# GNN stack on one core: one-hots of a message group in two halves, left-overs added one step later

## What is computed

```python
s = s @ (w_lin1_s / sqrt(MUL)); v = einsum('nui,uw->nwi', v, w_lin1_v / sqrt(MUL))
w = silu(edge_scalars @ fc_w1') @ fc_w2'          # w0, w1, w2, w3: 32 columns each
se = s[edge_src]; ve = v[edge_src]; es = edge_attr[:, :1]; ev = edge_attr[:, 1:4]
mid_s0 = w0 * se * es
mid_s1 = w3 * einsum('eui,ei->eu', ve, ev) / SQRT3
mid_v0 = (w1 * se)[:, :, None] * ev[:, None, :]
mid_v1 = (w2 * es)[:, :, None] * ve
ns = segment_sum(concat([mid_s0, mid_s1]), edge_dst); nv = segment_sum(concat([mid_v0, mid_v1]), edge_dst)
```

## Time and profile before

| what | us |
|---|---|
| median of 3 runs (8615.7 to 8623.8) | 8616.8 |
| profiled execution, own time | 8619.5 |
| span of its records | 8617.7 |
| message pass, from the first group's products to the last reduce | 1300 to 2353 |
| busy in the span: POOL / DVE / PE / ACT | 6169 / 5708 / 5622 / 3353 |
| mean granted TensorE clock, share of full | 0.76 |

### The profile page before, as it was taken

The page is one execution under the profiler, slowest core; times in us unless marked ns, Lnnn a source line. Parts: engine busy times, 40 slices in busy tenths (PEclk is TensorE's granted clock), DMA queues, the critical chain, the costliest instruction groups (busy, mean ns, idle before and its releaser), DMA issues. The chain is left out here.

```text
span 8617.7 us, 105909 instructions
## 1 busy us (share of the span) xinstructions
PE 5622.0 (65%) x23206; PEld 3921.9 (46%) x23206; DVE 5707.8 (66%) x15405; ACT 3352.8 (39%) x10636; POOL 6169.0 (72%) x6427
## 2 busy tenths in 40 slices
PE   5576646666666665777766666666655555788885
PEld 3343323444344443444444444444444444666664
DVE  8938308888866666666666666555544444788987
ACT  2232326777645553333323343000001111566665
POOL 2878767777577776777777777777777777666664
PEclk6555557777788888999989998788865555788886
DMA  2111115443322223444444443644433332211111
GB/s 71 46 57 46 54 62 142 112 113 109 90 76 63 64 63 108 119 118 119 119 138 119 119 119 114 141 117 115 116 97 62 62 62 60 51 48 49 49 49 38
DMA packets 632225, 749.12 MB, mean 87 GB/s; under 512 B 257060, under 2 KB 490168, under 8 KB 631464
## 3 DMA queue, kind: packets, MB, share of 16 engines
q0 software_dynamic: 239808, 572.66, 23.3%
q1 hardware_dynamic: 391512, 169.55, 7.8%
q10 hardware_dynamic: 272, 0.14, 0.0%
HBM read 617.05 MB, written 124.77 MB: 86 GB/s over the span
## 5 line engine op out<-in xcount | busy, mean ns | idle before, releaser
L815 DVE TENSOR_TENSOR acc<-acc,ps 128x256 f32 (+3 forms) x4704 | 1765.2, 375 | 1640.9 <-PE ps L1857 1259.2
L1140 POOL DMA_INDIRECT rows<-table_gcn,index_dst x1984 | 1887.5, 951 | 672.3 <-issue 577.1
L1857 PE MATMUL ps<-rows,hot 128*128 128x256 f32 (+2 forms) x5536 | 1499.2, 407 | 1254.8 <-DMA rows<-table_gcn,index_dst 487.7
L1857 PEld LDWEIGHTS ps<-rows,hot 128*128 128x128 f32 x5536 | 1096.2, 244 | 1647.6 <-issue 723.7
L1751 ACT ACTIVATE ut<-u,fld 128x128 f16<-128x128 f16 x1568 | 541.9, 392 | 1527.5 <-DVE u L1799 1526.7
L1140 POOL DMA_INDIRECT rows<-table_gat,index_dst x832 | 785.1, 944 | 375.3 <-issue 238.2
L1140 POOL DMA_INDIRECT rows<-table_lin,index_dst x784 | 739.7, 944 | 300.3 <-issue 230.4
L1140 POOL DMA_INDIRECT rows<-table_mean,index_src x784 | 741.3, 945 | 249.3 <-issue 232.3
L1109 PE MATMUL ps<-prod,hot 128*128 128x257 f32 x1568 | 625.0, 533 | 404.1 <-DVE prod L1062 318.1
L1842 PE MATMUL ps<-prod,ut 128*128 128x392 f16 x3136 | 740.4, 365 | 0.0
L1140 POOL DMA_INDIRECT pay<-table_gcn,index_dst x576 | 548.7, 953 | 175.4 <-issue 163.6
(11 more groups left out here) (428 smaller groups left out, 11012.3 us busy)
## 6 DMA issues: line engine op xcount, KB each, us to landing
fld<-dst_rows SPq DMA_DIRECT2D x98, 544.0 KB
rows<-table_gcn,index_dst POOLq DMA_INDIRECT x1984
table_gcn<-acc SPq DMA_DIRECT2D x147, 128.0 KB
fld<-left_rows SPq DMA_DIRECT2D x147, 128.0 KB
pay<-dst_rows SPq DMA_DIRECT2D x832, 1.0 KB
rows<-table_gat,index_dst POOLq DMA_INDIRECT x832
rows<-table_lin,index_dst POOLq DMA_INDIRECT x784
rows<-table_mean,index_src POOLq DMA_INDIRECT x784
```

Of the source, the lines that this page charges most:

```text
L815: c.nc.vector.tensor_tensor(to, to, product, ALU.add).then_inc(c.added.sem, 1)
L1140: pool.indirect_dma_start(to(q, j), None, table, bass.IndirectOffsetOnAxis(ap=c.idx[k][:, t:t + 1], axis=0)).then_inc(c.gathered[q % per]. ...
L1857: pe.matmul(c.ps[:, bank(q, j), 0:used], c.hot[:, r % 2, j, :], row_of(c, s, r, j, used), start=True, stop=True).then_inc(c.mm.sem, 1)
```

## The change

The one-hots of a group are made in two compares of 128 x 512 elements, one for each half, each right behind step 0 (the dot product) of the products of its half. Each counts `hot_ready` once, so every wait on it now counts two per group: TensorE's stands before each half instead of before the group; the SP queue's load of group q waits for both halves of group q - 4; GpSimd waits for the last of all. The one-hots of a half wait for TensorE to be through with the same half of group q - 2. The mask is made in halves as well (4 columns). The add of a left-over (`left_add`) comes behind the product step that follows its chunk's add and no longer ahead of it.

```diff
@@ load
-                    c.hold(sp, c.hot_ready, c.hot_ready.n + q - RING + 1)
+                    c.hold(sp, c.hot_ready, c.hot_ready.n + 2 * (q - RING + 1))
@@ hot
-            def hot(i, r):
+            def hot(i, r, b):
                 q = RING * i + r
-                dve.wait_ge(m.pay[r].sem, i * 16 + (m.pay[r].n + 16))
+                js = slice(4 * b, 4 * b + 4)
+                places = s.pay4[:, r, js, LO:LO + 1]
+                if b == 0:
+                    dve.wait_ge(m.pay[r].sem, i * 16 + (m.pay[r].n + 16))
                 if q >= 2:
-                    dve.wait_ge(c.mm.sem, c.mm.n + done((q - 1) * G8))
+                    dve.wait_ge(c.mm.sem, c.mm.n + done((q - 2) * G8 + 4 * b + 4))
...
-                one_hot(c, r % 2, places)
+                nc.vector.tensor_tensor(c.hot[:, r % 2, js, :], c.ps[:, PLACES, 0:P].unsqueeze(1).broadcast_to([P, 4, P]),
+                                        places.broadcast_to([P, 4, P]), ALU.is_equal).then_inc(c.hot_ready.sem, 1)
@@ reduce
                 products(i, r, 1, 0)
+                hot(i, r, 1)
                 for j in range(4):
                     layer.dve(dve, q * G8 + j)
                     add(q, j, bins[j])
                     products(i, r, 1, j + 1)
+                    add_left(q * G8 + j)
                 if after(i, r, 1, RING):
-                    hot(*after(i, r, 1, RING))
-
                     products(*after(i, r, 1, RING), 0, 0)
+                    hot(*after(i, r, 1, RING), 0)
                 for j in range(4, G8):
                     layer.dve(dve, q * G8 + j)
                     add(q, j, bins[j])
                     if after(i, r, 1, RING):
                         products(*after(i, r, 1, RING), 0, j - 3)
+                    add_left(q * G8 + j)
@@ product
-                pe.wait_ge(c.hot_ready.sem, q + (c.hot_ready.n + 1))
                 for j in range(G8):
                     if j % 4 == 0:
+                        pe.wait_ge(c.hot_ready.sem, c.hot_ready.n + 2 * q + j // 4 + 1)
                         pe.wait_ge(m.prod.sem, q * 2 + (m.prod.n + j // 4 + 1))
```

More of the change, by code:

```diff
@@ L1003, in _ @@
             pool.wait_ge(m.kept.sem, m.kept.n + NG)
-            pool.wait_ge(c.hot_ready.sem, c.hot_ready.n + NG)
+            pool.wait_ge(c.hot_ready.sem, c.hot_ready.n + 2 * NG)
             pool.iota(s.wide, pattern=[[1, NCH]], base=0, channel_multiplier=0, allow_small_or_imprecise_dtypes=True)
@@ L1009, in _ @@
         def _(dve):
-            def hot(i, r):
+            def hot(i, r, b):
                 q = RING * i + r
-                dve.wait_ge(m.pay[r].sem, i * 16 + (m.pay[r].n + 16))
+                js = slice(4 * b, 4 * b + 4)
+                places = s.pay4[:, r, js, LO:LO + 1]
+                if b == 0:
+                    dve.wait_ge(m.pay[r].sem, i * 16 + (m.pay[r].n + 16))
                 if q >= 2:
-                    dve.wait_ge(c.mm.sem, c.mm.n + done((q - 1) * G8))
-                places = s.pay4[:, r, :, LO:LO + 1]
+                    dve.wait_ge(c.mm.sem, c.mm.n + done((q - 2) * G8 + 4 * b + 4))
                 if q < LEFT_GROUPS:
[L1018 to L1021, removed]
-                one_hot(c, r % 2, places)
+                    places = s.hidden[:, q % 2, js].unsqueeze(2)
+                    nc.vector.tensor_tensor(places, s.pay4[:, r, js, LO:LO + 1],
+                                            c.outside[:, q * G8 + 4 * b:q * G8 + 4 * b + 4].unsqueeze(2),
+                                            ALU.add).then_inc(m.masked.sem, 1)
+                    dve.wait_ge(m.masked.sem, m.masked.n + 2 * q + b + 1)
+                nc.vector.tensor_tensor(c.hot[:, r % 2, js, :], c.ps[:, PLACES, 0:P].unsqueeze(1).broadcast_to([P, 4, P]),
+                                        places.broadcast_to([P, 4, P]), ALU.is_equal).then_inc(c.hot_ready.sem, 1)
             def products(i, r, b, step):
@@ L1069, in add, with add_left @@
                 add_item(c, dve, item(t), bin_, AU, c.ps[:, bank(q, j):bank(q, j) + 1, 0:AU])
+            def add_left(t):
                 if t in LEFT_AT:
@@ L1090, in reduce @@
                         products(*after(i, r, 1, RING), 0, j - 3)
+                    add_left(q * G8 + j)
             wait_places(c, dve)
-            hot(0, 0)
+            hot(0, 0, 0)
             for step in range(5):
@@ L1117, in messages @@
     end_pass(c, RING, G8)
+    c.hot_ready.n += NG
     end_left(c, 32)
@@ L1120, in messages @@
     c.idx_ready.n += NG
-    m.masked.n += LEFT_GROUPS
+    m.masked.n += 2 * LEFT_GROUPS
     for r, p in enumerate(m.pay):
```

## The result

The changed kernel takes 8651.2 us (7 runs, 8647.4 to 8656.2) against 8620.9 of the kernel before beside it: ratio 1.0036, 95% interval 1.0024 to 1.0047. It is slower by 30 us, 0.36%; the forecast was 8597, with 8622 at the far end of the range.

What follows compares the result with a forecast made beforehand. The message stage was taken as a loop of VectorE and TensorE, with the load chain beside it. Terms -31 - 6 + 14 + 3 = -20 us took 8619.5 to 8599.5, as a median 8597; forecast 8585 to 8607, range 8573 to 8622.

Steps and rivals of the forecast that it cites:

- Term 1: Message stage, VectorE: one-hots in two halves gain 0.40 us a group over 77 groups, 31 us, bounds 12 and 42.
- the second kind of half: Halves of a group that held the one-hots, 4.65 us without a wait; claimed to become 4.12 at 2.4 GHz.
- the 9.81: Us a group now: halves without one-hots average 4.76, those with them 5.05, no layer or left-over work.
- s = 0.6: Assumed share of halves at TensorE's low clock; a group takes 8.48 + 1.56 s, so 9.41 us.
- The share of the low clock: TensorE at 1.2 GHz about half of the time, 0.7 in halves without one-hots; 0.6 assumed after the change.
- Rival 1: TensorE's low clock takes over: every half 5.02 us, a group 10.04, total 8646 us; chance 0.12 of over 17 us slower.
- Term 2: Left-overs' adds moved behind one product step: 6 us gained, bounds 0 and 12, mostly where last in a half.
- Term 3: Sync queue, first groups: load waits for the second one-hots, delaying the left-over stores behind it; 14 us lost, bounds 0 and 20.
- Term 4: Later groups: the same load goes out later, so ScalarE waits for it; 3 us lost, bounds 0 and 15.
- the prediction's signs: What the next profile must show, among them ScalarE's wait for the load up from 20.8 us to 100 or more.

Runs made afterwards that it cites:

- e2: The kernel before with only the left-overs' adds moved one step later: 8604.3 us, ratio 0.9982.
- e4: The changed kernel with one-hots compared with places ScalarE has copied, so the load of a group need not wait for them: 8620.1 us, ratio 1.0003.
- e6: e4 with two buffers for the dot product's intermediate, one for each half: 8611.4 us, ratio 0.9986.
- e5: e4 with each half of the one-hots ahead of the dot product of its half: 8564.1 us, ratio 0.9936.
- e3: The changed kernel with the first of each pair of left-over stores ahead of the load in the sync queue: 8629.1 us, ratio 1.0010.
- e7: The kernel before with one-hots compared with places ScalarE has copied, so the load does not wait for them: 8620.6 us, ratio 1.0000.
- e9: The changed kernel with each half of the one-hots ahead of its dot product, the load still waiting for both: 8574.6 us, ratio 0.9947.

## Why the prediction was wrong

The runs give a chain that adds up to the 22.8 us of the pass: the left-overs' adds -11.4 (before to e2), the halving with the load free +7.4 (e2 to e4), the load's wait +26.8 (e4 to the changed kernel). Against the forecast's -6, -31 and 14 + 3 the miss of 43 us lies almost all in the halving. Taken out in another order the shares differ: in the changed kernel the left-overs' adds are worth 1.

- **Term 1, the halved one-hots, has the wrong sign, and this is the step that failed.** It said of the second kind of half at 2.4 GHz "4.65 - 1.14 + 0.61 = 4.12". That takes out the one-hots and leaves the dot product 0.50 us behind the reduce, where the one-hots had been; where it follows a reduce directly the distance is 0.71 to 0.72, and the prediction itself counts 0.72 in its sum for 1.2 GHz. It is the dot product's wait for the reduce that reads the same buffer; the one-hots had hidden it in one half of two, and e6, which takes this wait away by a second buffer, brings the distance to 0.50. Among the plain halves (groups 8 to 97, without layer or left-over work on VectorE) none in the changed kernel is shorter than 4.35 us. The shortest of the two kinds were 4.07 and 4.65 before, so even at best a group gains 0.02 us and not 0.24. Work rose by 18.3 us instead of the 7 that 0.08 us a group gives. The idle before adds and left-overs fell by 38, as hoped for, but went into work and into the dot product's wait (22.5), and so to nothing.
- **The rest of the 31 us was in the numbers that the term was compared with.** With 4.35 in place of 4.12 its formula still gives 9.5 us a group and 23 us gained. But the 9.81 that it starts from includes groups 1 to 7, which the term leaves out: in groups 8 to 97 plain halves average 4.74 and 4.91 us, 9.65 together. And s = 0.6 was a choice; at the 0.7 of the kernel before the corrected formula gives 9.64, no gain at all. Measured are 10.02 us in the changed kernel, 9.89 in e4 and 9.05 in e5. The idle time that the one-hots were to fill stayed in these halves: 1.0 us a group before, 1.0 in e4, 1.2 in the changed kernel, and only e5 has 0.5.
- **The share of the low clock** was no cause that shows. Over 1400 to 2280 us the granted clock was 0.77 in the changed kernel and 0.76 in e4 and before. Halves of over 4.8 us did become more frequent (45 of 61, before 46 of 73). Rival 1 gave 8646, near the result, and 10.04 us a group, near the 10.02, by a mechanism that the runs do not bear out: e3, e4 and e5 move the time by 22 to 87 us by the order of the queue and of VectorE alone. That its number is near is luck.
- **Term 2** (6) was too small when alone: 11.4 in the pass, 13 in the median, at the upper bound. In the changed kernel it is 1, in e5 it is 11.
- **Term 3** (14) was right in mechanism and place; the load left 1.45 us behind the dot product as worked out, but from the load's issue to the store's landing it is 6.7 to 7.1 us and not 6.0, which makes 20.4, the far bound (17 to 19 by e3 and e4). The one back-to-back case of the profile, 7.2, had been the right number; taking 1.2 off it was wrong.
- **Term 4** (3) measured 8 in the second part (976.9 to 969.1 in e4) and 9 between the medians of e3 and e4, inside its bounds of 0 and 15; the second parts of the kernel before and of e7, equal in time, differ by 5. ScalarE's wait grew to 166 us, as the prediction's signs had it (100 or more); at e9's order the same kind of wait costs nothing.

## What to carry to other kernels

When work is moved away from behind an instruction, look at what the next instruction then waits for: a wait for the engine's own last result shows as a longer distance between starts and in no idle column. Filler that depends on nothing late belongs ahead of the instruction that waits, not behind it; here the same two compares cost 16 us behind the dot product (e4 against e2) and save 40 and more ahead of it (e5 against e2). And a hold that two conditions share is free only while one of them is always early; before one is moved, follow what stands behind the hold in the same queue.

## What was not expected of the hardware

A store of 514 KB issued 0.4 to 0.7 us behind a load of 544 KB in the same queue landed 6.0 to 6.7 us after its issue, against 3.5 to 4.4 where no load had gone out in the 1.7 us ahead of it (nine stores of the kernel before). In e5 TensorE got through more matmuls in the same stretch at a granted clock of 0.83 instead of 0.76. That the earlier VectorE brought the higher clock is not shown, and how much of the 56 us is the clock was not separated.
